# Stack rows filled straight from the pieces, and a new order for the start and the first two batches

## What is computed

```python
h = tokenizer(x)                          # 3 colours -> 1, relu curve, clip: 8 x 256 x 256
h = concatenate([h, txt], axis=1)         # 384 tokens of 256
n = layernorm(h)
c = n @ W_DKV; k = c @ W_UK; v = c @ W_UV; q = n @ W_UQ
s = where(causal, q k^T / 4, -inf)        # 16 heads
h = h + softmax(s) v @ W_O
n = layernorm(h)
for k in (0, 1):                          # top 2 of 8 experts, capacity 384 tokens each
    h = h + weight_k * expert_k(n)        # 256 -> 1024 -> gelu -> 256
```

## Time and profile before

| | us |
|---|---|
| median of 3 runs | 739.59 (734.21 to 741.02) |
| the profiled execution | 733.21 |
| its span, first to last instruction | 731.4 |
| TensorE busy in it | 652.9 |
| VectorE (DVE) busy | 405.6 |
| ScalarE (ACT) busy | 378.8 |
| GpSimd (POOL) busy | 306.9 |
| mean granted TensorE clock, share of full | 0.969 |

### The profile page before, as it was taken

One profiled execution on the slowest core, in us unless ns is written; L12 is line 12 of the kernel. 1 busy time (PEld: TensorE's weight loads), 2 busy tenths in 40 slices (PEclk: granted clock), 3 DMA queues, 4 the chain that ended last, 5 costly groups with the idle time before them and its releaser, 6 DMA issues. The chain is left out here.

```text
span 731.4 us, 14563 instructions
## 1 busy us (share of the span) xinstructions
PE 652.9 (89%) x5586; PEld 546.8 (75%) x5586; DVE 405.6 (55%) x1010; ACT 378.8 (52%) x799; POOL 306.9 (42%) x393
## 2 busy tenths in 40 slices
PE   2766899989989899899998959999999999999992
PEld 2444556666656667666676849999999999999992
DVE  6547467677787877766864525444444444444220
ACT  3426475765748558375644035554454455554440
POOL 6100000100313212131314529888888877778233
PEclk9989999999999999999999979999999999999997
DMA  7477748280643616239101253254444444442223
GB/s 256 151 174 201 186 129 227 58 203 25 177 107 87 170 34 178 61 93 273 55 26 66 75 166 116 44 126 117 119 104 102 102 102 102 102 102 45 22 27 39
DMA packets 56582, 83.16 MB, mean 114 GB/s; under 512 B 5056, under 2 KB 48586, under 8 KB 56512
## 3 DMA queue, kind: packets, MB, share of 16 engines
q1 hardware_dynamic: 45440, 66.99, 33.1%
q0 software_dynamic: 9216, 12.41, 10.2%
q10 hardware_dynamic: 1856, 2.82, 1.2%
HBM read 50.50 MB, written 31.78 MB: 113 GB/s over the span
## 5 line engine op out<-in xcount | busy, mean ns | idle before, releaser
L1552 DVE TENSOR_TENSOR hl<-h,hh 128x384 fp32r<-128x384 f32 x128 | 103.7, 811 | 155.7 <-ACT h L1509 155.5
L1043 DVE TENSOR_REDUCE mx<-s_bank 128x2 f32<-128x256 f32 (+2 forms) x192 | 124.4, 683 | 66.7 <-PE s_bank L575 65.7
L1506 ACT ACTIVATE hh<-t_bank 128x384 fp32r<-128x384 f32 x128 | 63.0, 492 | 133.1 <-PE t_bank L1594 130.8
L869 ACT ACTIVATE pt<-t_bank 128x512 f32<-128x512 f32 x128 | 76.4, 597 | 72.9 <-PE t_bank L598 71.9
L1475 POOL DMA_INDIRECT out<-yo,xr x48 | 74.8, 1557 | 71.9 <-ACT yo L1517 62.2
L1463 POOL TENSOR_TENSOR wl<-wr,wh 128x256 fp32r<-128x256 f32 x112 | 94.7, 879 | 1.2
L597 PE MATMUL t_bank<-qs,ks 98*128 98x384 bf16 (+2 forms) x384 | 86.3, 277 | 4.7 <-DMA qs<-mT 4.0
L1594 PE MATMUL t_bank<-xh,wh 128*128 128x384 f32 x256 | 86.8, 339 | 0.0
L1594 PE MATMUL t_bank<-xl,wh 128*128 128x384 f32 x256 | 86.4, 338 | 0.0
L1594 PE MATMUL t_bank<-xh,wl 128*128 128x384 f32 x256 | 86.2, 337 | 0.0
L574 PE MATMUL s_bank<-ks,qs 96*128 96x128 bf16 (+2 forms) x384 | 80.5, 279 | 5.6 <-DVE mx L1043 5.2
(11 more groups left out here) (190 smaller groups left out, 1465.0 us busy)
## 6 DMA issues: line engine op xcount, KB each, us to landing
wr<-in_w SPq DMA_DIRECT2D x16, 1024.0 KB, 5.8
qk_scratch<-part SPq DMA_DIRECT2D x96, 96.0 KB
slot_rows<-empty SPq DMA_DIRECT2D x6, 1040.0 KB, 10.5
xr<-slot_rows SPq DMA_DIRECT2D x16, 390.0 KB, 3.3
wr<-in_x SPq DMA_DIRECT2D x6, 768.0 KB, 7.4
qs<-qk_scratch SPq DMA_DIRECT2D x16, 288.0 KB, 4.6
ks<-qk_scratch SPq DMA_DIRECT2D x16, 288.0 KB, 5.8
qs<-qk_scratch SPq DMA_DIRECT2D x16, 192.0 KB, 4.7
```

The costliest lines, as they stand in the source:

```text
L869: ins = act.activation(pt[:, p, unit // 2, 0:AT[1]], bank, ACT.Exp)
L1043: ins = dve.tensor_reduce(mx[:, p // 2, j, 2 * (p % 2):2 * (p % 2) + 2], pair_region(s_bank, j), AX_X, ALU.max)
L1506: act.activation(hh[:, f, :], h_banks[f % NH], ACT.Gelu_apprx_tanh)
L1552: dve.tensor_tensor(hl[:, f, :], h[f % 2][:, :], hh[:, f, :].bitcast(F32), ALU.subtract).then_inc(hl_done, 1)
```

## The change

`qk_scratch`, `spill` and `load_stack` go. A piece is copied from SBUF to SBUF, straight to every place of the stack that needs it: six copies of 96 KB for each of q and k of a half, 24 in a batch. So that one copy can do the turn from heads to depths, the host now lays the columns of W_UQ and W_UK depth first, and the rows of a stack interleave the pieces: row 6d + at holds depth d of pair number at. The rest:

- The keys' copies of the first half of batch 0 (k = 1) are issued by POOL, with a semaphore of their own; the others by SP.
- Minus ones: POOL and DVE no longer write them to `ks` with memsets on two partitions; POOL sets one tile `less`, and ACT issues four transfers from it. `minus_s` and `curve_w` are made by POOL.
- The first image is the first transfer on SP's queue, the parameters the first on ACT's; SP waits for the image before it issues the matrices and the second image. ACT does one small activation before the image is there.
- SP issues the zero rows in four transfers, in turns 0 to 3, and none before the loop.
- Batches 0 and 1: DVE does all six colour steps of batch 1 before the keys of batch 0, and its curve between them; ACT does the relus of batch 1 between the queries of batch 0. The transposes of batch 1 move into turn -1, step 0, behind the first plain scores, its latents into step 1. Queries and keys of its first half stay in turn -1, those of the second half move to turn 0. turning(60), behind the first relu, becomes turning(64), behind the third; turning(40) becomes turning(24).

```diff
+        def stack(queue, b, k, stage, landed=None):
+            half, s = k // 2, k % 2
+            dst = (ks if s else qs)[b % 2][half]
+            queue.wait_ge(*part_made(b, k, stage))
+            if b >= 2 and stage == 0:
+                queue.wait_ge(t_ready, 12 * (2 * (b - 2) + half + 1))
+            for at, piece in enumerate(K_PARTS if s else Q_PARTS):
+                if piece == stage:
+                    queue.dma_start(dst[at:MROW:len(Q_PARTS)], part[k][stage][:, :]).then_inc(landed or stack_in[half], 16)
...
-            sp.dma_start(prm[:, :], rows_to_all(params, NPRM)).then_inc(prm_in, 16)
+            load_x(0)
+            sp.wait_ge(x_in[0], 16)
             sp.dma_start(mat[:, 0:MAT_WO], mats[:, 0:MAT_WO]).then_inc(mats_in, 16)
+            load_x(1)
             sp.dma_start(mat[:, MAT_WO:NMAT], mats[:, MAT_WO:NMAT]).then_inc(rest_in, 16)
+            sp.dma_start(hid[:, 1:B, NT - 1, :], txt[1:B].rearrange("b p d -> p b d")).then_inc(text_in[1], 16)
             load_x(2)
-            for i in range(2):
-                empty_rows(i)
...
+            for i in range(3):
+                stack(sp, 0, 0, i)
+            for i in range(3):
+                for k in (2, 3):
+                    stack(sp, 0, k, i)
...
+            for i in range(3):
+                stack(pool, 0, 1, i, stack_soft)
             rstds(1)
...
-                    pe.wait_ge(stack_in[half], 16 * NL * (b + 1))
+                    pe.wait_ge(stack_in[half], stack_count(b, half))
+                    if n == 0:
+                        pe.wait_ge(stack_soft, 16 * len(K_PARTS))
...
-            pe.wait_ge(relu_done, 1)
-            turning(60)
+            pe.wait_ge(relu_done, CH)
+            turning(64)
...
-            turning(40)
-            for c in range(KC):
-                tokens_back(1, c, c)
+            turning(24)
             pe.wait_ge(rest_in, 16)
...
+            act.wait_ge(consts, 3)
+            act.activation(warm[:, :], eps_t[:, :], ACT.Identity).then_inc(warm_made, 1)
+            act.wait_ge(minus_made, 1)
+            for q in range(2):
+                for h in range(2):
+                    act.dma_start(ks[q][h][MROW:SROWS, :, :].rearrange("r h t -> r (h t)"), less[:, :]).then_inc(minus_in, 16)
...
                 if b:
-                    act.wait_ge(spilled[k // 2], 16 * 6 * b)
+                    act.wait_ge(stack_in[k // 2], stack_count(b - 1, k // 2))
...
-            for i, (k, stage) in enumerate(kk for kk in EARLY_ORDER[0] if kk[0] % 2):
-                if i < 3:
-                    colours(1, i + 1)
-                keys(0, k, stage)
-            for i in range(4, 6):
+            for i in range(6):
                 colours(1, i)
-            curve(1)
+            keys(0, 1, 0)
+            curve(1, (0,))
+            keys(0, 1, 1)
+            curve(1, (1,))
+            keys(0, 3, 0)
+            keys(0, 1, 2)
+            curve(1, (2,))
+            keys(0, 3, 1)
+            keys(0, 3, 2)
```

## The result

| | before | after |
|---|---|---|
| median, us | 737.92 (734.21 to 741.02, 4 runs) | 716.84 (715.48 to 718.17, 4 runs) |
| the profiled execution | 733.21 | 715.48 |
| its span | 731.4 | 713.6 |
| first plain scores / turn 0 / turn 1 start at | 43.73 / 60.77 / 79.66 | 33.32 / 44.97 / 64.27 |
| rows of the first expert | 428.94 | 411.70 |

The ratio is 0.9732, interval 0.9688 to 0.9776: 2.7% faster. The direction was forecast, the size was not. Of these 10.8 us, 5.7 are in the profile (715.5 against the 721.2 of the sum) and 5.0 in the step from one profiled execution to the median.

The account below looks back on a forecast made before the run. TensorE's chain up to the first expert's rows at 428.94 us bounds the kernel; 8.7 (start) + 4.5 (turn -1) - 1.2 (turn 0) = 12.0 gives 721.2, plus 6.4 to the median: 727.6 us, eight in 10 between 719.5 and 735.5.

Parts of the forecast that it names:

- the sum: Whole kernel: 8.7 + 4.5 - 1.2 = 12.0 us gained, 721.2 on the profiled execution's scale.
- Both halves: First plain scores: transpose order and way through DRAM together hold 43.73 us; removing one alone leaves the other.
- Term 1: Image and first colour steps: 0.5 us from small steps off DVE, the 1.43 us of three being "mostly latency".
- Term 2: Clock at 23 us, latents and queries: a shorter idle gap keeps the clock up, 1.7 us.
- Term 3: DVE up to the third key piece: six colour steps come first; piece at 29.8 against 31.7, 1.9 us survive.
- Term 4: Key pieces to stack: POOL's copies at 0.98 us each; scores start at 35.0 instead of 43.7, 8.7 us.
- Terms 5 and 6: Turn -1 loses 3.8 us of matmuls, lasts 12.5, gains 4.5; turn 0 takes them on, 20.5, minus 1.2.
- Term 7: Steady turns: 0 us, the copies' issuing on SP and their DMA packets being hidden.
- rival C: SP's queue becomes the bound if copies exceed 1.9 us; at 2.2 us each about 770 us; chance 0.05.
- rival D: Larger gain: parameters land earlier, POOL costs little, turn -1 near 10 us; 17 us, 722.6; chance 0.07.

Follow-up runs that it names:

- copies_alone: Kernel before with SBUF-to-SBUF copies on SP's queue instead of spills and loads; start, orders, zero rows and minus ones as before: 731.73 us, ratio 0.9939.
- before_look: The kernel before, unchanged, one execution on the fourth chip for a second profile: 757.97 us.
- before_filled: Kernel before with turning(130) instead of turning(40) ahead of batch 1's transposes: 734.66 us, ratio 0.9990.
- less_turning: Changed kernel with turning(20) instead of turning(64) and none instead of turning(24): 719.83 us, ratio 0.9773.
- after_third: The changed kernel, unchanged, run again on another chip: 733.78 us, ratio 0.9769 to the kernel before.

## Where the prediction failed, and what of it held

Two steps failed, and each put the forecast some five microseconds too high. The first is the step from the profiled execution to the median, taken over from the kernel before as 6.4 us, where the new kernel's is 1.4. The second is the sum: 12.0 us, where the span gave 17.8. The start gave 1.7 more than its terms, turn -1 0.9, turn 0 0.8, the steady turns 1.9, and what lies behind the first rows 0.6. What the gain is made of was right, and the terms were mis-sized; in term 1 the cause was wrong too.

**The question and the structure held.** The gain is the shift of the first scores and of turns -1 and 0, 15.4 of 17.8 us. Both halves are needed.

**Term 1 was mis-sized:** 1.5 us instead of 0.5. The steps off DVE gave 0.46, as priced. What failed is "mostly latency": the small steps ran beside POOL's memsets, and the removal of these memsets and the early table load were priced at nothing.

**Term 2 held** in its effect: the latents took 1.53, the clock read 1.00. Its reason is only in part borne out. In the twelve profiles with turning(64) behind the third relu TensorE idled at most 1.28 us ahead of the transposes, and the latents took 1.53 each time. In the seven with the start of before it idled 2.00 to 2.93, and they took 1.53 in three and 2.40 to 2.90 in four. Among these the idle time does not decide it: in `copies_alone` it was 2.63 and the clock did not fall; in `before_look` it was 2.00 and the latents took 2.90, with a clock of 0.67 from 20 to 25 us. What does stays open.

**Term 3** had the third key piece at 29.8, and it came at 28.23. All but 0.1 of the 1.6 us was there at the first piece, taken at 24.69 instead of 26.2: 1.0 is term 1, and the colour steps of batch 1 started another 0.4 earlier (20.71 for 22.1) and were 0.1 shorter. From there on the sum was right, 3.54 for 3.6.

**Term 4** gave 5.2 us from the third key piece to the scores, and 5.09 were measured, but by errors that cancel. POOL's copies took 0.53, not 0.98: a plain copy is like SP's, not like the indirect transfer that was chosen as "the nearest in shape". Then the last query copy and its landing ended last. The start as a whole gave 10.4 instead of 8.7.

**Terms 5 and 6:** turn -1 gave 5.4 for 4.5, turn 0 cost 0.4 for 1.2. The 3.8 us of matmuls moved as forecast. In turn -1 the matmuls were not over-priced (10.0 us, for 9.1): the waits between them were, at 1.7 us for the 3.4 that the sum "filled" in. In turn 0 it is the reverse: the matmuls took 15.8 us for 17.6, the waits 3.5 for 2.9. Part of that is the full clock (1.00, for the 0.91 of before), worth 1.7 us at 19.3 x 0.09, where the sum takes off 0.85 and gives no reason for the figure. The wait of 2.04 us for maxima rows has gone, as said.

**Term 7** was 0 and 1.9 came. Copies on SP's queue are hidden as forecast: 598 ns each in the median, and the two microseconds of rival C were reached by single ones only (2287 at most). The four profiles of the quicker chips with the way through DRAM need 349.3 to 351.2 us from turn 1 to the first rows, the six with direct copies 345.6 to 349.0, in the mean 350.2 and 347.8. That the copies save these 2.4 us is likely and not shown: no single wait accounts for them, and executions on the other chips scatter by more.

**The scale failed:** the largest single error. The profiled execution of before lay 6.4 us under the median of 739.6, and I carried this distance over to the new kernel as it stood. With a fourth run the median of before is 737.9, 4.7 above the profile; the new kernel's own distance is 1.4. The distance of one execution from the median is no property that passes from kernel to kernel: the one before spreads over 7 us, the changed one over 2.7. 5.0 of the 10.8 us come from here. Within one kernel the spread goes with the clock, and the profiled execution of before was one of high clock (0.969). Why the changed kernel's clock varies less stays open. It is not the idle time ahead of batch 1 (`before_filled` spreads over 8 us), nor the early zero rows, nor the end of the front.

**The chances:** rival D, the larger gain, had 0.07 and was nearest: its 17 us are what the profile gave (17.7), and only the scale made 722.6 of them. But that is mostly luck, for its reasons carried little: the parameters landed 0.2 us earlier, POOL's cheap copies did not move the scores beyond term 4, and turn -1 took 11.65 us, not 10. The low end of the range lacked a median that does not carry the old offset.

## What to carry to other kernels

Where two delays end together, price the removal of both, and test each alone: here 5.7 and 7.6 us became 20.1. A short step that takes three times its usual duration is not latency: look at what runs beside it on the other engines, and whether the two end together, before it gets a price. And leave the distance between a profile and the median out of the forecast, or put it into the range: it belongs to that execution's clock. Matmuls that only keep the clock up want a look at what starts when they end.

## What the runs showed of the hardware

- Beside memsets of POOL on 2 partitions (2x3072 bf16, two in 5.31 us) small steps of DVE ended only with the memset, 0.03 to 0.07 us behind it: three `curve_w` took 1.43 against 0.51 us, the reduction 1.02 against 0.18, `minus_s` 1.44 against 0.17.
- Issuing can hold an engine for microseconds: four transfers from `less` to two rows each, behind two images and the texts on ACT's queue, took 10.6 us to issue; in the changed kernel, with only the parameters and a text ahead, they were done by 7.00.
- Copies from SBUF to 16 spread partitions are cheap: 396 packets on SP's queue took 50.7% of sixteen engines in 2 us, 41 ns each, beside 43 for the spills to DRAM.
- The granted clock can read 1.00 while matmuls take twice their time (`less_turning`, 20 to 25 us, latents 2.90 for 1.53 us): the durations have to be read beside it.
- TensorE's own issue can fail it for 13 us in a row (gaps of up to 1.8 us between one to five matmuls, 10.1 us in all in `after_third`), on three of the chips and not on the others, at the same place of the program. With it, turn 1 to the first expert's rows took 357 to 371 us instead of 346 to 351.
